# Value products of a linear-memory attention layer: all heads as three f16 products

## What is computed

```python
scores = jnp.where(mask, -jnp.inf, jnp.einsum('bhid,bhjd->bhij', q, k) * scale)
att_dot = jnp.einsum('bhij,bhjv->bhiv', jax.nn.softmax(scores, axis=-1), v)
sq = jax.nn.elu(q) + 1.0
att_mem = sq @ M / (sq @ jnp.swapaxes(Z, -2, -1))
sk = jax.nn.elu(k) + 1.0
M_new = M + jnp.einsum('bhld,bhlv->bhdv', sk, v)
att = gate * att_mem + (1.0 - gate) * att_dot
out = att.reshape(B, LSEG, H * DV) @ Wo
```

## Time and profile before

| | us |
|---|---|
| median of 3 runs | 1027.13 (1026.92 to 1029.09) |
| the profiled execution | 1026.99 |
| its span, first to last instruction | 1025.2 |
| busy: TensorE, weight loads | 958.7, 677.2 |
| busy: VectorE, ScalarE, GpSimd | 825.9, 654.1, 614.8 |
| a middle step, between score products of group 0 | 50.7 |

### The profile page before, as it was taken

The page is one execution under the profiler, slowest core; times in us unless marked ns, Lnnn a source line. Parts: engine busy times, 40 slices in busy tenths (PEclk is TensorE's granted clock), DMA queues, the critical chain, the costliest instruction groups (busy, mean ns, idle before and its releaser), DMA issues.

```text
span 1025.2 us, 21046 instructions
## 1 busy us (share of the span) xinstructions
PE 958.7 (94%) x8004; PEld 677.2 (66%) x8004; DVE 825.9 (81%) x1464; ACT 654.1 (64%) x1428; POOL 614.8 (60%) x752
## 2 busy tenths in 40 slices
PE   5899999999999999999999999999999889999971
PEld 2577777777777777777777776777777755333430
DVE  5879798978888888879897978797979564588785
ACT  5757575658575755576666556757575554777872
POOL 3466767546666764476767635767676362456563
PEclk9999999999999999999999999999999899999995
DMA  7000000000000000000000000000000002200025
GB/s 195 33 21 2 22 2 21 2 22 1 22 2 22 2 22 1 21 2 22 2 22 1 22 1 22 2 22 2 12 2 29 7 12 80 94 1 0 1 49 116
DMA packets 17042, 23.97 MB, mean 23 GB/s; under 512 B 7472, under 2 KB 9264, under 8 KB 16432
## 3 DMA queue, kind: packets, MB, share of 16 engines
q1 hardware_dynamic: 15472, 18.58, 6.6%
q10 hardware_dynamic: 1472, 4.06, 1.2%
HBM read 13.97 MB, written 8.65 MB: 22 GB/s over the span
## 4 chain that ended last, share of the span: by engine, by line
PE 88%; DVE 5%; ACT 3%; issue 2%; POOL 1%; POOLq 0%; DVEq 0%
PE ps L1302 24%; PE ps L1424 11%; PE ps L1319 7%; PE ps L1381 6%; PE ps L1356 6%; PE ps L1366 5%; PE ps L1346 5%; PE ps L1569 4%; PE ps L1582 4%; PE ps L1396 3%; PE ps L1409 3%; PE ps L1564 3%; PE ps L1379 2%; PE ps L1334 2%; PE ps L1277 1%
## 5 line engine op out<-in xcount | busy, mean ns | idle before, releaser
L1302 PE MATMUL ps<-arena 128*128 128x512 f16 x1152 | 274.4, 383 | 5.5 <-DVE arena L938 3.1
L682 ACT ACTIVATE arena<-ps,arena 128x128 f32<-128x128 f32 x512 | 141.9, 375 | 116.6 <-DVE arena L985 116.6
L1302 PEld LDWEIGHTS ps<-arena 128*128 128x128 f16 x1152 | 109.7, 98 | 119.2 <-DVE arena L961 6.0
L961 DVE STREAM_TRANSPOSE arena<-ps 128x1024 f32<-128x1024 f32 x96 | 145.2, 1513 | 3.5 <-PE ps L1302 3.4
L1424 PE MATMUL ps<-arena 128*128 128x256 f32 x544 | 120.3, 380 | 0.0
L1424 PEld LDWEIGHTS ps<-arena 128*128 128x128 f32 x544 | 102.2, 190 | 13.8 <-ACT arena L702 0.8
L489 POOL TENSOR_TENSOR arena<-arena 128x260 f16<-128x260 f32 x64 | 42.7, 666 | 113.1 <-ACT arena L697 113.1
L478 POOL TENSOR_TENSOR arena<-arena 128x256 f32<-128x256 f32 x128 | 93.2, 728 | 19.4 <-DVE arena L1001 19.4
L482 POOL TENSOR_TENSOR arena<-arena 128x256 f32<-128x256 f32 x128 | 94.6, 739 | 10.0
L689 ACT ACTIVATE arena<-ps 128x512 f16<-128x512 f32 (+1 forms) x128 | 77.0, 602 | 36.2 <-PE ps L1356 36.0
L480 POOL TENSOR_TENSOR arena<-arena 128x256 f32<-128x256 f32 x128 | 93.3, 729 | 10.0
(11 more groups left out here) (125 smaller groups left out, 1996.4 us busy)
## 6 DMA issues: line engine op xcount, KB each, us to landing
x_rows<-arena SPq DMA_DIRECT2D x17, 256.0 KB, 2.0
arena<-x_rows SPq DMA_DIRECT2D x4, 1024.0 KB, 8.6
arena<-in_L_attn_x_dram SPq DMA_DIRECT2D x124, 32.0 KB, 1.7
out_dram<-arena SPq DMA_DIRECT2D x18, 128.0 KB, 3.0
arena<-in_L_attn_Wq_dram ACTq DMA_DIRECT2D x2, 512.0 KB, 4.7
arena<-in_L_attn_Wk_dram ACTq DMA_DIRECT2D x2, 512.0 KB, 6.3
arena<-in_L_attn_Wv_dram ACTq DMA_DIRECT2D x2, 512.0 KB, 7.8
arena<-in_L_attn_Wo_dram SPq DMA_DIRECT2D x8, 128.0 KB, 4.4
```

The source lines that it names most:

```text
L682: last = act.activation(Pr[:, par, j, :], s_bank[:, par, j * P:(j + 1) * P], ACT.Exp, bias=negm[:, par, j:j + 1])
L961: dve.transpose(dst[:, d0:d0 + 32], bank.rearrange("p w (d c) -> p d w c", c=C)).then_inc(x_free, 1)
L1302: last = pe.matmul(bank[:, w, :], xc[:, lx, k, w * P:(w + 1) * P], W16[lw][:, k, i, :], start=(n == 0), stop=(n == 5))
```

## The change

The odd heads' value products become three f16 products too. PT32 goes; PT16 holds high and low parts for both par; vsplit holds both heads' values, so v_high and v_low go over 520 columns instead of 260. low_p runs twice per group, once per par, and values and scores wait for both. values issues twelve f16 products per call. The lists of all four engines are rearranged. The diff below leaves out the rest of ScalarE's and TensorE's lists. TensorE's list from score product 1 on reads, after the change: scores(1), A2, A3, recall(0,1), values(0,1), remember(0), turn 2 Q, turn_probs(1,0), project_out, turn 2 K, turn_probs(1,1), recall(1,0), N, first half of project 2, values(1,0), its second half; scores(2), recall(1,1), values(1,1), remember(1), turn 3 Q, project 3, turn_probs(2,0), recall(2,0), turn 3 K, turn_probs(2,1), project 4, F, values(2,0); scores(3), recall(2,1), values(2,1), remember(2), turn 0 Q, turn_probs(3,0), first half of project 5, turn_probs(3,1), turn 0 K, its second half, recall(3,0), values(3,0). On ScalarE's list the later exp_q and v_high move ahead of or between the probabilities of their group.

```diff
-PT16 = alloc(GP * P, F16).rearrange("p (n j i) -> p n j i", n=2, j=GP)
-PT32 = alloc(GP * P).rearrange("p (j i) -> p j i", j=GP)
+PT16 = alloc(GU * P, F16).rearrange("p (h n j i) -> p h n j i", h=2, n=2, j=GP)
...
-vsplit = [alloc(UNITS // 2 * VE // 2, F16).rearrange("p (g h e) -> p g h e", g=GROUPS, h=GP)
+vsplit = [alloc(UNITS * VE // 2, F16).rearrange("p (g r h e) -> p g r h e", g=GROUPS, r=2, h=GP)
...
-        :, g // 2, 0, GP * (g % 2):GP * (g % 2) + GP, 0:DV1]
+        :, g // 2, :, GP * (g % 2):GP * (g % 2) + GP, 0:DV1]
...
-            hi, lo = (v[:, g, :, 0:DV1] for v in vsplit)
+            hi, lo = (v[:, g, :, :, 0:DV1] for v in vsplit)
             pool.tensor_tensor(lo, v_units(s, g), hi, ALU.subtract).then_inc(vl_done, 1)
...
             m = bp * NSEG + s
-            v_low(bp, s, 0)
+            elu_k(bp, s, 0)
             if m > 0:
                 gated(*before(bp, s), 3, 0)
                 gated(*before(bp, s), 3, 1)
-            elu_k(bp, s, 0)
+            v_low(bp, s, 0)
             elu_k(bp, s, 1)
             v_low(bp, s, 1)
-            gated(bp, s, 0, 0)
             if m < NT - 2:
                 deviation(n_rs, n_mv, n_stat, n_rstd, m + 3)
+            gated(bp, s, 0, 0)
+            v_low(bp, s, 2)
+            y_dev(bp, s)
+            residual(bp, s)
+            gated(bp, s, 0, 1)
+            x2_dev(bp, s)
+            gated(bp, s, 1, 0)
             elu_k(bp, s, 2)
-            y_dev(bp, s)
-            gated(bp, s, 0, 1)
-            residual(bp, s)
-            x2_dev(bp, s)
+            v_low(bp, s, 3)
             elu_k(bp, s, 3)
-            v_low(bp, s, 2)
-            gated(bp, s, 1, 0)
             gated(bp, s, 1, 1)
             gated(bp, s, 2, 0)
...
-            dst = PT16[:, 0] if par == 0 else PT32
             act.wait_ge(pt_full, bp * 32 + 8 * s + 2 * g + par + 1)
-            act.activation(dst.rearrange("p j i -> p (j i)"), s_bank[:, par, :],
+            act.activation(PT16[:, par, 0].rearrange("p j i -> p (j i)"), s_bank[:, par, :],
                            ACT.Copy).then_inc(p_copied, 1)
...
-            act.activation(vsplit[0][:, g, :, 0:DV1], v_units(s, g), ACT.Copy).then_inc(vh_done, 1)
+            act.activation(vsplit[0][:, g, :, :, 0:DV1], v_units(s, g), ACT.Copy).then_inc(vh_done, 1)
...
             exp_k(bp, s, 0)
             v_high(bp, s, 0)
             exp_q(bp, s, 1)
+            high_k(bp, s, 1)
             probs(bp, s, 0, 0)
             probs(bp, s, 0, 1)
             take_p(bp, s, 0, 0)
-            v_high(bp, s, 1)
             take_p(bp, s, 0, 1)
             if s == 0 and bp > 0:
                 reset(*before(bp, s), 3)
-            high_k(bp, s, 1)
-            exp_k(bp, s, 1)
             take_a(t_job(bp, s, "A0"), 0)
             take_a(t_job(bp, s, "A1"), 1)
+            exp_k(bp, s, 1)
+            take_a(t_job(bp, s, "A2"), 2)
             probs(bp, s, 1, 0)
-            take_a(t_job(bp, s, "A2"), 2)
             take_a(t_job(bp, s, "A3"), 3)
+            v_high(bp, s, 1)
...
-        def low_p(bp, s, g):
+        def low_p(bp, s, g, par):
             G = bp * 16 + 4 * s + g
-            hi, lo = (PT16[:, n].rearrange("p j i -> p (j i)") for n in range(2))
-            dve.wait_ge(p_copied, 2 * G + 1)
-            dve.tensor_tensor(lo, s_bank[:, 0, :], hi, ALU.subtract).then_inc(p_low, 1)
+            hi, lo = (PT16[:, par, n].rearrange("p j i -> p (j i)") for n in range(2))
+            dve.wait_ge(p_copied, 2 * G + par + 1)
+            dve.tensor_tensor(lo, s_bank[:, par, :], hi, ALU.subtract).then_inc(p_low, 1)
...
             if m > 0:
                 divide(*before(bp, s), 3, 1)
             take_q(bp, s, 1)
+            take_k(bp, s, 1)
             if not last:
                 take_x(bp, s, 0)
-            low_p(bp, s, 0)
             to_rows(bp * 32 + 8 * s + 8, (0,))
-            take_k(bp, s, 1)
             to_rows(bp * 32 + 8 * s + 8, (1,))
+            low_p(bp, s, 0, 0)
+            low_p(bp, s, 0, 1)
             divide(bp, s, 0, 0)
             maxima(bp, s, 1, 0)
             if ahead:
                 n_stats((s + 2) % 4, 128 * (bp + 1 + (s + 2) // 4), m + 3)
             maxima(bp, s, 1, 1)
+            divide(bp, s, 0, 1)
             if not last:
                 take_x(bp, s, 1)
-            low_p(bp, s, 1)
-            divide(bp, s, 0, 1)
-            take_q(bp, s, 2)
             if ahead:
                 n_norm((s + 2) % 4, m + 3)
+            take_q(bp, s, 2)
+            low_p(bp, s, 1, 0)
             y_stats(bp, s)
+            low_p(bp, s, 1, 1)
             take_k(bp, s, 2)
             y_norm(bp, s)
+            divide(bp, s, 1, 0)
             if not last:
                 take_x(bp, s, 2)
+            x2_stats(bp, s)
+            maxima(bp, s, 2, 0)
             if ahead:
                 split(t_job(bp, s, "N"), s % 2, m + 3)
-            divide(bp, s, 1, 0)
-            maxima(bp, s, 2, 0)
-            x2_stats(bp, s)
             maxima(bp, s, 2, 1)
+            divide(bp, s, 1, 1)
             if not last:
                 take_x(bp, s, 3)
             x2_norm(bp, s)
-            divide(bp, s, 1, 1)
-            low_p(bp, s, 2)
             take_q(bp, s, 3)
+            low_p(bp, s, 2, 0)
+            low_p(bp, s, 2, 1)
             take_k(bp, s, 3)
+            seq_sums(bp, s)
             divide(bp, s, 2, 0)
             maxima(bp, s, 3, 0)
             maxima(bp, s, 3, 1)
             if not last:
                 take_x(bp, s, 4)
             divide(bp, s, 2, 1)
-            seq_sums(bp, s)
-            low_p(bp, s, 3)
+            low_p(bp, s, 3, 0)
             if not last:
                 take_q(bp, s, 0)
+            low_p(bp, s, 3, 1)
+            if not last:
                 take_k(bp, s, 0)
             divide(bp, s, 3, 0)
             if not last:
...
-                pe.wait_ge(p_copied, 2 * (bp * 16 + G))
-                pe.wait_ge(p_low, bp * 16 + G)
+                pe.wait_ge(p_low, 2 * (bp * 16 + G))
...
-            v = v_pos[s % 2].rearrange("p (y r h e) -> p y h r e", y=2, r=2, h=HP)[:, g // 2]
-            pe.wait_ge(p_copied, 2 * (G + 1))
-            pe.wait_ge(p_low, G + 1)
+            pe.wait_ge(p_low, 2 * (G + 1))
             pe.wait_ge(vl_done, G + 1)
-            for a in range(2):
-                j = 2 * half + a
+            for u in range(4):
+                j, par = 2 * half + u // 2, u % 2
                 for i, (lp, lv) in enumerate(((0, 0), (0, 1), (1, 0))):
-                    pe.matmul(pm_bank[:, 0, 2 * a * DV1:(2 * a + 1) * DV1], PT16[:, lp, j, :],
-                              vsplit[lv][:, g, j, 0:DV1], start=(i == 0), stop=(i == 2))
-                last = pe.matmul(pm_bank[:, 0, (2 * a + 1) * DV1:(2 * a + 2) * DV1], PT32[:, j, :],
-                                 v[:, GP * (g % 2) + j, 1, 0:DV1], start=True, stop=True)
+                    last = pe.matmul(pm_bank[:, 0, u * DV1:(u + 1) * DV1], PT16[:, par, lp, j, :],
+                                     vsplit[lv][:, g, par, j, 0:DV1], start=(i == 0), stop=(i == 2))
             if half == 0 or s == NSEG - 1:
                 last.then_inc(pm_full, 1)
...
                 remember(*before(bp, s), 3)
             turn(bp, s, 1, "Q")
             if not last:
-                project(bp, s, 0)
+                project(bp, s, 0, (0,))
             turn(bp, s, 1, "K")
+            if not last:
+                project(bp, s, 0, (1,))
+            recall(bp, s, 0, 0)
             turn_probs(bp, s, 0, 0)
-            recall(bp, s, 0, 0)
             turn_probs(bp, s, 0, 1)
             if not last:
                 project(bp, s, 1)
+            turn_att(t_job(bp, s, "A0"), 0, nat_n)
+            turn_att(t_job(bp, s, "A1"), 1, nat_n)
             values(bp, s, 0, 0)
             scores(bp, s, 1)
-            turn_att(t_job(bp, s, "A0"), 0, nat_n)
-            turn_att(t_job(bp, s, "A1"), 1, nat_n)
+            turn_att(t_job(bp, s, "A2"), 2, nat_n)
+            turn_att(t_job(bp, s, "A3"), 3, nat_n)
             recall(bp, s, 0, 1)
-            turn_att(t_job(bp, s, "A2"), 2, nat_n)
             values(bp, s, 0, 1)
-            turn_att(t_job(bp, s, "A3"), 3, nat_n)
             remember(bp, s, 0)
             turn(bp, s, 2, "Q")
             turn_probs(bp, s, 1, 0)
             if m == 0:
                 pe.wait_ge(c_in, 128)
             project_out(t_job(bp, s, "Y"), [t_job(bp, s, a) for a in ("A2", "A3")])
+            turn(bp, s, 2, "K")
             turn_probs(bp, s, 1, 1)
```

More of the change, by code:

```diff
@@ L733, in step @@
                         reset(*before(bp, s), 3)
-                    high_k(bp, s, 1)
-                    exp_k(bp, s, 1)
                     take_a(t_job(bp, s, "A0"), 0)
                     take_a(t_job(bp, s, "A1"), 1)
+                    exp_k(bp, s, 1)
+                    take_a(t_job(bp, s, "A2"), 2)
                     probs(bp, s, 1, 0)
-                    take_a(t_job(bp, s, "A2"), 2)
                     take_a(t_job(bp, s, "A3"), 3)
+                    v_high(bp, s, 1)
```

(49 more changed lines are left out.)

1 line of the change is left out of this document (removed).

## The result

The changed kernel takes 1042.83 us in the median of three executions (1040.94 to 1045.92) beside 1027.13 before: a ratio of 1.0149, 95% interval 1.0115 to 1.0183. The profiled execution took 1040.94 (span 1039.1), 14 us more than before.

A forecast was written before the change was run, and what follows sets the result against it. TensorE and VectorE were both taken as full, so little of TensorE's 39 us saving would count: -2.4 (twelve steps), -4.5 (three with s = 3), -1.5 (last), sum -8.4 from 1026.99, median 1018.7 us; range 1004 to 1037.

The forecast's parts named there:

- stretch B: From a step's score product 1 to 2, with the output projection: TensorE limits it, 17.92 to 16.4 us, -1.5.
- Stretch A: From a step's score product 0 to 1: VectorE's added low part delays score product 1, 11.57 to 12.9 us, +1.3.
- must all end before values(0,0): Between score products 0 and 1: VectorE's old items plus one low part end at 12.3 us, holding the value call.
- rival 4: TensorE gaps lower its clock: 1030 in a few steps, at most 1070; other order mistakes 1040; together chance 0.10.
- Stretch C: From a step's score product 2 to 3: VectorE's line shrinks to 11.4 us, the stretch stays 11.8, no change.
- x2_norm's first half slips in at the end of the first addition: Between score products 2 and 3: x2_norm waits only for GpSimd's second addition, 1.55 us instead of 2.34; margin 0.15.
- rival 1: Between score products 2 and 3, x2_norm meets two GpSimd instructions: 2.8 instead of 1.55 us, total 1033; chance 0.27.
- Stretch D: From score product 3 to the next step's 0: VectorE-bound, 9.45 us again; 8.6 in steps with s = 3.
- Seq_sums and divide(2,0) fill that wait: After score product 3: they use VectorE's 0.48 us wait for it, so the added low part leaves 9.45 us unchanged.
- 8.6: Microseconds from score product 3 to the next step's 0 at s = 3: 9.45 less 0.85 for absent second-half additions.
- Rival 3: TensorE's whole saving counts, as if VectorE's unbroken lines did not matter: 988 us; chance 0.03.
- Outside the steps nothing changes: Work ahead of and behind the sixteen steps keeps its time: no term in the sum.

The follow-up runs named there:

- e6_rows: Changed kernel with group 0's low parts ahead of to_rows on VectorE, A0 and A1 behind score product 1, exp_k(1) earlier on ScalarE: 1045.26 us, ratio 1.0177.
- e2_pad: Changed kernel with one more tiny, unneeded GpSimd operation ahead of elu_k(2): 1034.79 us, ratio 1.0064.
- e1_swap: Changed kernel with GpSimd's elu_k(2) moved ahead of gated(1,0): 1034.93 us, ratio 1.0061.
- e5_seq: Changed kernel with seq_sums split: reduction behind divide(2,0), 4-column addition in the next step, between the second and third score products: 1034.65 us, ratio 1.0074.
- e10_norows: Changed kernel with the edits of e5_seq and e7_act, plus ScalarE's v_high(3) and x2_norm moved earlier: 1015.94 us, ratio 0.9878.
- e11_swap_seq: Changed kernel with the edits of e1_swap and e5_seq together: 1022.09 us, ratio 0.9944.
- e7_act: Changed kernel with the steps' x2_norm moved from VectorE to ScalarE as a scaled, shifted copy, GpSimd making the shift: 1040.67 us, ratio 1.0128.

## Why the forecast was wrong

The forecast for the profiled execution was 1018.6; it took 1040.94, 22.3 more. By the table of stretches: C +13.6, D +10.4, A -1.0, B -1.7, together 21.3; ahead of the first step -1.5; the last step, forecast at -1.5, came with the end to +1.0, so +2.5. That makes 22.3.

- **What bounds the kernel, TensorE's saving and stretch B: right.** B was 16.26 (forecast 16.4), with TensorE busy in all of it.
- **Stretch A came out by some luck.** It was 12.6 (forecast 12.9, which the prediction's own terms make 12.8), but the step "must all end before values(0,0)" isn't what held it: TensorE's own line, put at 11.9, needs 12.14 us of work and waits 0.38 for ScalarE's probabilities, which the sum left out and rival 4 names among its other mistakes. e6_rows, which takes VectorE's low parts out of the way, gains nothing. At s = 0, for which I took the same +1.3, A grew more: 10.75 to 12.66.
- **Stretch C failed in the step "x2_norm's first half slips in at the end of the first addition".** The place, the mechanism and both prices were about right: 1.61 measured for the case I chose (e2_pad; 1.55 in the sum), 2.54 against 2.8 for rival 1. But I chose by a margin of 0.15 us out of 12 us of counting, and the count was 0.17 off between the two engines, so the kernel fell on the other side. e1_swap and e2_pad touched GpSimd alone, the second only by giving it more to do, and C fell to 11.9 and 12.1, beside the 11.8 I forecast. A margin as small as the sum's own error of counting should have had a chance of one half; rival 1 had 0.27.
- **Stretch D failed in two steps.** "Seq_sums and divide(2,0) fill that wait" counted seq_sums as its duration and left out that its 4-column addition, with both operands in SBUF (arena in the rows), meets GpSimd as x2_norm does: 0.5 us in eight steps, 4.2 us in all. Two clock spells of 1.2 each came behind the waits. e5_seq, which moves the addition, has neither; that the waits cause the spells is argued and not shown, since six like them had none. And "8.6" at s = 3 was scaled from other steps: the trace of before had 9.72 there, which I didn't cut out. The change puts the sums, which wait for take_f, ahead of divide(2,0), and that made it 10.04: 1.4 in three steps, 4.3 us. By 9.56 in e5_seq, which moves the sums behind divide(2,0), about a third of that is this order; what holds the rest no run settles.
- **Rival 4 was partly right**: waits of 0.9 us were followed by the lower clock in two steps, at 1.2 us each in the profiled execution. Rival 3 is out: with C freed from VectorE altogether (e10_norows) the kernel still stops at 1015.94.
- **With C and D put right the forecast's sum comes out, in part because misses cancel**: the fifteen steps of e11_swap_seq take 747.4, where the forecast makes 747.6, with A and B 2.8 under their forecasts and C and D 2.6 over. Its 1022.09 lies 3.4 over the forecast: the last step and the end took 4.2 more than forecast, the work ahead of the first step 0.5 less.
- **"Outside the steps nothing changes" failed too.** In the last step the stretches A to C went from 38.33 us to 36.82, the 1.5 of the forecast, though at a mean clock of 1.00 beside 0.91 before. What follows that step's last score product grew by 2.5 us in the changed kernel and 2.6 in e11_swap_seq, with a spell of the lower clock at 849.47 and at 837.87 that the kernel before hasn't there. What makes up the rest no run settles.

The Trainium skill (page "SBUF — State Buffer", section "Who interferes with whom") says that a VectorE instruction with two SBUF inputs contends with a GpSimd instruction that reads SBUF. The rows of the 4-column addition agree: 0.17 us alone, 0.67, 1.13 and 1.23 beside GpSimd. The same section gives the ports to whichever issues first. x2_norm's record in stretch C begins 0.06 us before GpSimd's addition and still waited for it, so the starts in the records don't decide that order.

## What to carry to other kernels

Before giving work to an engine that shares something with another, list every instruction of both that meets there, the tiny ones too, and price each by the length of the longest instruction that it can meet. Where a count decides a case by less than 0.2 us, treat it as undecided, and look for an order that doesn't depend on it: a different neighbour, a place with slack, or another engine. When work is moved to an idle engine, follow what stands behind it in that engine's list: e7_act's gain was lost to a copy that had nothing to do with the change.
